# Four instead of eight feature tiles in the plain part of a gated feed-forward layer, and its preparing jobs split between two engines

## The reference, cut to what matters

```python
xn = layernorm(x)                      # x: 8 blocks x 512 rows x 512
s = state_space_mixer(xn)              # not touched here
h = rmsnorm(xn) * ln2
mod = 0.1 * tanh(attention(xn) @ A)    # attention is not touched here
gate = silu(h @ W_in_base.T + mod * (h @ A) @ B)      # 2048 features
up = h @ W_up_base.T
f = xn + (gate * up) @ W_down.T
out = x + s * silu(f)
```

## Time and profile before

| | |
|---|---|
| runs | 2474.39, 2479.31, 2480.7 us; median 2479.31 |
| profiled execution | 2479.31 us, of which the span (first to last instruction) is 2477.3 us |
| busy in the span | PE 2400.3 us (97%), DVE 1498.7 (60%), ACT 1108.8 (45%), POOL 708.8 (29%) |
| plain part after the attention | from about 1441 to 1958.5 us of the span |
| second part, 16 steps | from 1958.5 us to the end |
| granted clock of PE | 0.988 in the mean |

### The profile page before, as it was taken

One profiled execution on the slowest core, in us unless ns is written; L12 is line 12 of the kernel. 1 busy time (PEld: TensorE's weight loads), 2 busy tenths in 40 slices (PEclk: granted clock), 3 DMA queues, 4 the chain that ended last, 5 costly groups with the idle time before them and its releaser, 6 DMA issues.

```text
span 2477.3 us, 37647 instructions
## 1 busy us (share of the span) xinstructions
PE 2400.3 (97%) x13847; PEld 1944.4 (78%) x13847; DVE 1498.7 (60%) x3000; ACT 1108.8 (45%) x1895; POOL 708.8 (29%) x674
## 2 busy tenths in 40 slices
PE   7999999999999899999999999999999999999998
PEld 5878878778888777777777678888888887787876
DVE  7857667667565588888988853223332345454546
ACT  6444544544444377777777641111111233332333
POOL 4000000000001244454453616664647002121212
PEclk9999999999999999999999899999999999999999
DMA  4000100000003577676666426655555945555461
GB/s 146 18 35 1 35 18 18 35 18 18 17 1 107 184 208 215 201 201 192 178 182 201 129 77 208 217 198 188 194 199 175 351 174 205 203 189 219 163 245 68
DMA packets 190747, 348.65 MB, mean 141 GB/s; under 512 B 19008, under 2 KB 89664, under 8 KB 181840
## 3 DMA queue, kind: packets, MB, share of 16 engines
q1 hardware_dynamic: 188064, 345.91, 42.6%
q10 hardware_dynamic: 2496, 0.29, 0.1%
HBM read 234.70 MB, written 111.15 MB: 140 GB/s over the span
## 4 chain that ended last, share of the span: by engine, by line
PE 80%; DVE 7%; issue 5%; DMA 4%; ACT 2%; POOL 2%; SPq 1%; DVEq 0%; ACTq 0%; POOLq 0%
PE PS L72 12%; PE PS L74 12%; PE PS L73 12%; PE PS L1748 3%; PE PS L813 2%; PE PS L812 2%; PE PS L814 2%; PE PS L2253 2%; PE PS L2254 2%; PE PS L2255 2%; PE PS L1706 2%; PE PS L1725 2%; PE PS L1707 2%; PE PS L1708 2%; PE PS L2612 2%
## 5 line engine op out<-in xcount | busy, mean ns | idle before, releaser
L1912 DVE CUSTOM_DVE_ANT_0 PS<-PS,MK 128x512 f32<-128x512 f32 (+3 forms) x512 | 244.4, 503 | 70.5 <-PE PS L1725 68.7
L1848 ACT ACTIVATE PF<-PS 128x512 f32<-128x512 f32 (+1 forms) x384 | 201.0, 528 | 90.5 <-PE PS L1752 60.0
L2302 DVE TENSOR_TENSOR SG<-SG,PS 128x512 f32<-128x512 f32 x60 | 41.3, 688 | 290.9 <-PE PS L74 289.7
L72 PE MATMUL PS<-XH,WH 128*128 128x512 f32 x504 | 208.8, 414 | 0.0
L74 PE MATMUL PS<-XH,WL 128*128 128x512 f32 x504 | 197.6, 392 | 0.0
L73 PE MATMUL PS<-XL,WH 128*128 128x512 f32 x504 | 196.8, 390 | 0.0
L74 PE MATMUL PS<-FH,GU 128*128 128x512 f32 x480 | 187.9, 391 | 0.0
L73 PE MATMUL PS<-FL,GU 128*128 128x512 f32 x480 | 187.5, 391 | 0.0
L72 PE MATMUL PS<-FH,GU 128*128 128x512 f32 x480 | 187.4, 390 | 0.0
L1725 PE MATMUL PS<-KS,QS 96*128 96x512 f32 (+3 forms) x512 | 172.4, 352 | 13.2 <-DVE MX L1912 13.1
L72 PE MATMUL PS<-XB,SW 128*128 128x512 f32 x448 | 175.5, 392 | 4.4 <-ACT P L2669 3.6
(11 more groups left out here) (352 smaller groups left out, 6644.5 us busy)
## 6 DMA issues: line engine op xcount, KB each, us to landing
SW<-sw_scratch SPq DMA_DIRECT2D x10, 3584.0 KB, 12.3
qk_scratch<-QT SPq DMA_DIRECT2D x128, 256.0 KB, 4.7
QS<-qk_scratch SPq DMA_DIRECT2D x96, 256.0 KB, 4.0
KS<-qk_scratch SPq DMA_DIRECT2D x96, 256.0 KB, 4.0
xt_scratch<-JOB SPq DMA_DIRECT2D x32, 512.0 KB, 3.5
XB<-xt_scratch SPq DMA_DIRECT2D x16, 1024.0 KB, 6.3
sw_scratch<-JOB SPq DMA_DIRECT2D x32, 448.0 KB, 3.3
DW<-dw_scratch SPq DMA_DIRECT2D x10, 1024.0 KB, 5.0
```

Source lines behind the costliest of these rows:

```text
L72: pe.matmul(o, lh(k), xh(k), start=open_ and k == 0, stop=False, skip_group_check=True)
L1848: act.activation(PE_[u][:, o:o + at], PS[4 + a % 2][:, 0:at], ACT.Exp, scale=SC).then_inc(a_ex, 1)
L1912: dve.tensor_tensor_reduce(out=p, in0=p, in1=MK[:, 512 - n:512], scale=1.0, scalar=NEG, op0=ALU.add, op1=ALU.max, accum_out=MX[w % 2][:, j ...
```

## The change

The plain part takes feature tiles 0 to 3 only: four columns a block, 32 in all, of which 4 to 31 follow the attention. The second part takes tiles 4 to 15: six units instead of four, 24 steps instead of 16. Slices 4 to 7 go.

The jobs are split: Pool makes the weights of units 0 to 4 and all six outward jobs (26 jobs), DVE all rows and the weights of unit 5 (20 jobs). Each engine has two JOB buffers and semaphores of its own. Every column from 5 on carries a Pool job, and three of four a DVE job, which follows the column's product in DVE's order. A job's store and the load of the engine's job after the next stand one behind the other in the list.

In the second part one modulation product goes to the bank of the first down tile instead of ZG, and the waits of the first down tiles follow. Buffers change places; SW0 now lies where nothing of the plain part is, so that its first load has no wait of its own.

```diff
-        GU.append(sb(re_, "GU1", [128, 4, 4, 512], F32R))
+        sb(re_, "GAP", [128, 8192])
...
+        JOB += [sb(js, f"JOB{i}", [128, 2048], F32R) for i in (2, 3)]
...
-        PAIRS, UNITS = NB // 2, 4
+        PAIRS, UNITS, FIRST = NB // 2, 6, 4
...
-        jobs = [job for u in range(UNITS) for job in rows_jobs[u] + unit_jobs[u]]
+        jobs = [[], []]
+        for u in range(UNITS):
+            jobs[0] += (weight_jobs[u] if u < UNITS - 1 else []) + [("outward", u, 0, 0)]
+        jobs[1] = rows_jobs[0] + rows_jobs[1] + weight_jobs[UNITS - 1] + rows_jobs[2] + rows_jobs[3]
...
-            yield "slice", 4
             yield "sums", 4 * NB - 1
-            yield "slice", 5
             yield "rows", 1
             yield "skips", 0
...
-            yield "slice", 6
+            yield "skips_scaled", 0
+            for w in range(2):
+                for n in range(2):
+                    yield "job_load", (w, n)
             yield "down", 3
-            ahead = 0
-            for q in range(EARLY + 1, 8 * NB):
-                b, f = divmod(q, 8)
+            done = [0, 0]
+            for q in range(EARLY + 1, FIRST * NB):
+                b, f = divmod(q, FIRST)
                 yield "column", q
                 yield "product", q
                 yield "down", q - 1
                 if f == 0 and b + 1 < NB:
                     yield "rows", b + 1
...
-                if q >= 8 and q % 3 and ahead < len(jobs):
-                    if ahead == 0:
-                        yield "job", 0
-                    if ahead + 1 < len(jobs):
-                        yield "job", ahead + 1
-                    yield "job_kept", ahead
-                    ahead += 1
+                for w in range(2):
+                    if done[w] < len(jobs[w]) and (w == 0 or f < 3):
+                        yield "job", (w, done[w])
+                        yield "job_kept", (w, done[w])
+                        if done[w] + 2 < len(jobs[w]):
+                            yield "job_load", (w, done[w] + 2)
+                        done[w] += 1
...
+                elif kind == "job" and q[0] == 1:
+                    do_job(dve, *q)
...
-        def load_job(sp, n):
-            kind, a, j, k = jobs[n]
-            J = f32(JOB[n % 2][:, :])
+        def load_job(sp, w, n):
+            kind, a, j, k = jobs[w][n]
+            J = f32(JOB[2 * w + n % 2][:, :])
             if n >= 2:
-                sp.wait_ge(j_st[n % 2], j_st0[n % 2] + 32 * (n // 2))
+                sp.wait_ge(j_st[2 * w + n % 2], j_st0[2 * w + n % 2] + 32 * (n // 2))
...
-            for r in range(2):
-                sp.wait_ge(j_st[r], j_st0[r] + 32 * len(range(r, len(jobs), 2)))
-            sp.wait_ge(m_u, 56)
+            for r in range(4):
+                sp.wait_ge(j_st[r], j_st0[r] + 32 * len(range(r % 2, len(jobs[r // 2]), 2)))
+            sp.wait_ge(m_u, FIRST * NB - FIRST)
...
-                pe.wait_ge(n_ad, n_ad0 + 5 * v + 1)
-                modulate(pe, ZG, f1, b1, True).then_inc(n_pr, 1)
+                pe.wait_ge(*((n_ev, 8 * v - 3) if v else (m_fn, 4 * NB - 1)))
+                modulate(pe, DN[0], f1, b1, True).then_inc(n_pr, 1)
...
-                    if t < 2:
-                        pe.wait_ge(*((n_ev, 8 * v - 3 + t) if v else (m_fn, 4 * NB - 1 + t)))
+                    if t == 0:
+                        pe.wait_ge(n_ad, n_ad0 + 5 * v + 3)
+                    elif t == 1:
+                        pe.wait_ge(*((n_ev, 8 * v - 2) if v else (m_fn, 4 * NB)))
                     elif t < 4:
-                        pe.wait_ge(n_ad, n_ad0 + 5 * v + 5 - t)
+                        pe.wait_ge(n_ad, n_ad0 + 5 * v + t - 1)
```

More of the change, by code:

```diff
@@ L2085, in build @@
+        n_sw, n_sw0, n_dw, n_dw0 = m_wf, [64, 64], [m_dh, m_do], [4, 4]
         wd_ = WdT.rearrange("(f p) m -> f p m", p=128)
-        PAIRS, UNITS = NB // 2, 4
+        PAIRS, UNITS, FIRST = NB // 2, 6, 4
         ORDER = [u if p % 2 == 0 else UNITS - 1 - u for p in range(PAIRS) for u in range(UNITS)]
         rows_jobs = [[("rows", p, k, t) for k in range(2) for t in range(2)] for p in range(PAIRS)]
-        unit_jobs = [[("weights", u, j, k) for j in range(2) for k in range(2)] + [("outward", u, 0, 0)] for u in range(UNITS)]
@@ L2263, in ffn_scalar @@
             for kind, q in work:
[L2264 to L2273, removed]
+                if kind == "modulation":
                     attn_scalar(act, [("bounded", q, None), ("modulation_out", q, None)])
@@ L2325, in ffn_pool, with job_loads, job_ops @@
                     attn_pool(pool, [("inverse", n, None)])
-                elif kind == "job":
-                    do_job(pool, n)
+                elif kind == "job" and n[0] == 0:
+                    do_job(pool, *n)
             second_pool(pool)
[L2330 to L2336, removed]
-        def load_job(sp, n):
-            kind, a, j, k = jobs[n]
-            J = f32(JOB[n % 2][:, :])
+        def job_loads(w, n):
+            return sum(64 if jobs[w][i][0] == "rows" else 32 for i in range(n % 2, n + 1, 2))
+        def job_ops(w, n):
+            return sum({"rows": 7, "weights": 8, "outward": 2}[jobs[w][i][0]] for i in range(n + 1))
+        def load_job(sp, w, n):
+            kind, a, j, k = jobs[w][n]
+            J = f32(JOB[2 * w + n % 2][:, :])
             if n >= 2:
-                sp.wait_ge(j_st[n % 2], j_st0[n % 2] + 32 * (n // 2))
+                sp.wait_ge(j_st[2 * w + n % 2], j_st0[2 * w + n % 2] + 32 * (n // 2))
             else:
@@ L2372, in keep_job @@
                 to = [f32(dw_d[a])[:, :, x, :] for x in range(2)]
[L2373 to L2382, removed]
+            sp.wait_ge(j_op[w], j_op0[w] + job_ops(w, n) - 1)
@@ L2383, in do_job @@
+            sp.dma_start(to[0], high).then_inc(j_st[2 * w + n % 2], 16)
+            sp.wait_ge(j_op[w], j_op0[w] + job_ops(w, n))
+            sp.dma_start(to[1], low).then_inc(j_st[2 * w + n % 2], 16)
+        def do_job(e, w, n):
+            kind, a, j, k = jobs[w][n]
+            R_, J = JOB[2 * w + n % 2][:, :], f32(JOB[2 * w + n % 2][:, :])
+            done = job_ops(w, n - 1) if n else 0
+            e.wait_ge(j_ld[2 * w + n % 2], j_ld0[2 * w + n % 2] + job_loads(w, n))
             if kind == "rows":
@@ new lines, in do_job @@
+                e.tensor_tensor(w1, w1, l2, ALU.mult).then_inc(j_op[w], 1)
+                e.wait_ge(j_op[w], j_op0[w] + done + 2)
+                e.tensor_tensor(s1, a21, a22, ALU.add).then_inc(j_op[w], 1)
+                e.wait_ge(j_op[w], j_op0[w] + done + 3)
+                e.tensor_tensor(s2, s1, a11, ALU.subtract).then_inc(j_op[w], 1)
+                e.wait_ge(j_op[w], j_op0[w] + done + 4)
+                e.tensor_tensor(s4, a12, s2, ALU.subtract).then_inc(j_op[w], 1)
+                e.tensor_tensor(a21, a11, a21, ALU.subtract).then_inc(j_op[w], 1)
@@ L2431, in load_unit @@
         def load_unit(sp, u, free):
-            if free is None:
-                sp.wait_ge(m_u, 60 if u == 0 else 8 * NB)
-            else:
+            if free is None and u:
+                sp.wait_ge(m_u, FIRST * NB)
+            elif free is not None:
                 sp.wait_ge(n_pr, 15 * (free + 1))
@@ L2760, in second_pool @@
                 if v and v % UNITS == 0:
-                    for n in range(2 * v - 8, 2 * v):
+                    for n in range(8 * (v // UNITS) - 8, 8 * (v // UNITS)):
                         skipped(n)
```

189 lines of the change are left out of this document (84 added, 105 removed).

## The result

The changed kernel takes 2663.53 us in the median (2661.0 to 2667.54), the kernel before 2480.01 beside it: ratio 1.0745, 95% interval [1.073, 1.076]. Forecast were 2620 us in a range of 2552 to 2672: slower as predicted, by 183.5 us instead of 141. The profiled execution took 2665.2 us, its span is 2663.4.

What follows compares the result with a forecast made beforehand. Matmuls on PE bound the kernel before; after the change SP's queue would. From 2477.3 us: second part starting at 1846 instead of 1958.5, plus 248.1, 0.5, 5 and 2.0, gives 2620 us; range 2552 to 2672 (0.8), own range 2575 to 2670.

Steps and rivals of the forecast that it cites:

- Its signs: Plain part: PE near 60% busy, some 40 own-store waits, DMA above 0.8 at 270 to 290 GB/s; steps 31.0 us.
- Matmuls: Both parts: 32 columns leave, 270.1 us, and 8 steps come, 248.1 us; by PE alone -22.0 us.
- At the start: Column 4 now needs the second block's rows earlier; their load 0 to 1 us late, 0.5 taken.
- The jobs, transfers: Job stretch of the plain part: 98.6 MB through the DMA engines at 345 GB/s, 286 us.
- The jobs, waits: Job stretch: 42 of 46 jobs have a reload wait with about 1.8 us in which nothing moves, 75 us.
- The turn: Between the parts: PE, run dry, waits for all of the second part's first loads, 19.6 us.
- The first step: Second part's first step: 3 us waiting for the fourth block and 2 us more for PE's lower clock.
- the last stores: End of the job stretch: the last two jobs are computed and their stores land, some 8 us.
- slower matmuls: Plain part: PE's lower clock (0.50) after idling falls into waits there, so no time was added for it.
- in series: Job stretch: transfers of 286 us and reload waits of 75 us add up to 361 us.
- 2457 by PE alone: Faster rival: PE stays the bound through all 27 columns since loads are two jobs ahead, 2457 us; chance 0.03.
- the theory ahead of the high halves' run: Job stretch, loads ahead: transfers alone set it, 234 us instead of 303; second part 55 to 69 us earlier.

Runs made afterwards that it cites:

- loads first: Changed kernel with each reload issued ahead of that column's stores, into the buffer whose stores were issued a column or more earlier: 2555.25 us, ratio 1.0314.
- both together: Changed kernel with reloads issued ahead of the stores and the weights' scratch laid out for 3.5 KB store runs: 2543.88 us, ratio 1.0261.
- Longer runs: Changed kernel with the weights' scratch laid out so stores write 3.5 KB runs per partition instead of seven of 512 bytes: 2659.24 us, ratio 1.0737.
- the jobs with 142 us less of them: Changed kernel with most job instructions working on 16 columns instead of 256 to 1024, DMAs and waits the same: 2665.4 us, ratio 1.0758.
- the high halves' run: Changed kernel with reloads issued ahead of stores, low halves not stored and the high half loaded in their place: 2529.3 us, ratio 1.0206.
- the smaller step of the change: Six instead of four plain feature tiles, jobs split over Pool and DVE, reloads ahead of stores: 2471.0 us, ratio 0.9969 to the kernel before.

## Why the prediction was right, and where its terms were off

The mechanism was the one forecast: with jobs crowded into 27 columns, SP's queue sets the pace, through reloads that wait for stores just issued, and PE stands still behind DVE's waits. Its signs are there but for one: PE at 64% in the plain part, DVE waiting for loads, 42 own-store waits, steps of 31.0 us, and PE idle 21.7 us before the first. The one that was wrong: the DMA share is 0.73 at 235 GB/s, not above 0.8 at 270 to 290, and that shows the mis-sized terms. What went unsaid is that the waits come from the order of the list, which the change had turned round, more than from the crowding: loads first alone gives 108 of the 183.5 us back. Step by step:

- *Matmuls:* right. A step still is 31.0 us (the new modulation bank costs nothing), and from its first matmul to the end the second part lasts 768.6 us (2663.4 - 1894.8), a first step included that is 2.4 us longer; 766.9 were forecast without that. At the start PE shows no wait (0.5 forecast).
- *The jobs, transfers:* 286 us at 345 GB/s were forecast; measured are 302 us, 97.2 MB at 322 GB/s (235 / 0.73). With the weights' stores in short runs the rate of a full queue is 327, with long ones 349 (loads first, and both together). The 345 was the middle of windows of 336 and 353. The second of them held no weights' stores; the first held two of them and by its share is 336 / 1.04 = 323, the nearer value. +16 us.
- *The jobs, waits:* 42 by 1.8 us, 75 us, were forecast; the queue is idle 111 us, 2.6 a wait. The 1.8 came from a queue with one store in it. Here another engine's stores or loads are ahead of the awaited one, a weights store takes 5.7 us to land in the median (the row below, from 1457 to 1870 us; 3.3 in the earlier trace rows), and all of it is waited out. +36 us. This is the term that was most wrong, and 2.6 lies outside the 1.3 to 2.3 of the forecast's own range; the time stayed in that range, near its upper end, as the rate (322) was inside its tenth. Longer runs showed that it is no fixed price for a wait: most of what the transfers lost there, the waits gained.

```profile
sw_scratch<-JOB SPq DMA_DIRECT2D x48, 448.0 KB, 5.7
```

- *The turn:* 19.6 us forecast, 19.7 measured (1875.0 to 1894.8). PE now waits for the whole of it, as forecast.
- *The first step:* 5 us forecast, 2.4 measured. PE shows no wait for the fourth block; some 4.6 us at the lower clock level account for the 2.4.

Sum of the errors: 16 + 36 for the jobs, 3 less for the last stores (5 us from the stretch's end at 1870 to the loads at 1875.0, 8 forecast; the last issue itself ends at 1868.2), 2.6 less for the first step: 46 us. The span exceeds the forecast's 2618 by 45. The 37 us of slower matmuls have no place in this sum: most of them fell into waits, as forecast.

The forecast held that in the changed kernel DVE's and Pool's instructions play no part: shown by the jobs with 142 us less of them. It put transfers and waits "in series": taking the waits away took away 108 us and left 300 us of transfers, so the series holds there; as a law of two fixed addends it does not, see above. That the rest with the loads first (2555 against 2457 by PE alone) is transfers alone, as the theory ahead of the high halves' run had it, was wrong: of 69 us of transfers taken out, 26 came back. What holds the rest was not tried.

## What to carry to other kernels

In a queue that issues in program order, put the reload of a buffer ahead of stores just issued, not behind them: each load behind its own store drains the queue, here 2.6 us a time. Before work moves off the bottleneck, divide what has to hide (bytes by the rate of a full queue, jobs by their length) by what is left to hide it in: 302 us of transfers don't hide under 228 us of matmuls, 282 do under 355, and the smaller step of the change was the one that gained, with its loads first. When a cheaper transfer or instruction brings nothing, look for the wait that contains it.

## What was not expected of the hardware

- Stores of 448 KB in runs of 512 bytes lowered the rate of the whole full queue from 349 to 327 GB/s, and yet long runs brought no more than 4 us of 2660, within the noise, where landings were awaited.
- After 21.7 us without work PE's matmuls came 0.43 us apart, the lower of its two levels (1.2 GHz), until 1899, then 0.228 apart at the upper one (2.4 GHz); granted were 0.93 in the mean of that first step. In the job stretch the same falls behind nearly every wait of PE, some 37 us of PE's time in all. The prediction had counted it as hidden, and the record supports that without a run of its own: DVE waited for PE 13.6 us in that stretch and for its jobs' loads 215, and the sum above comes out without the 37.
- While the second part's first loads, with four stores of 256 KB among them, and the first step ran together, the DMA engines moved 420 GB/s; over a whole job stretch, with the jobs' stores among the transfers, 328 was the most.
